# Expert layers of a transformer kernel: gate and up as three fp32r products instead of one fp32 product

## The reference

```
x = x + 0.5 * expert_ffn(layernorm(x))
x = x + attention(layernorm(x))
x = x + 0.5 * expert_ffn(layernorm(x))
x = x + 0.5 * sparse_ffn(layernorm(x))
x = x + mamba(layernorm(x))
x = x + 0.5 * sparse_ffn(layernorm(x))
```

```
logits = 30 * tanh(x @ w_gate / 30);  probs = softmax(logits)
weights = probs where the expert is among the token's top 2, else 0
for e in range(8):
    h = silu(x @ w1[e]) * (x @ w3[e])        # w1, w3: 256 x 512 ("gate" and "up")
    out = out + h @ w2[e] * weights[:, e]    # w2: 512 x 256 ("down")
```

## Time and profile before

| what | value |
|---|---|
| median of 3 runs | 1663.79 us (1658.72 to 1665.37) |
| the profiled execution | 1661.38 us, its span 1659.6 us |
| PE busy | 1454.4 us, 88% |
| DVE busy | 1085.8 us, 65% |
| ACT busy | 847.5 us, 51% |
| POOL busy | 487.5 us, 29% |
| mean granted TensorE clock | 0.938 of 2.4 GHz |
| the two expert layers, from first gate to last down | 137.7 and 137.8 us |

### The profile page before, as it was taken

One profiled execution on the slowest core, in us unless ns is written; L12 is line 12 of the kernel. 1 busy time (PEld: TensorE's weight loads), 2 busy tenths in 40 slices (PEclk: granted clock), 3 DMA queues, 4 the chain that ended last, 5 costly groups with the idle time before them and its releaser, 6 DMA issues. The chain is left out here.

```text
span 1659.6 us, 24358 instructions
## 1 busy us (share of the span) xinstructions
PE 1454.4 (88%) x7712; PEld 1014.0 (61%) x7712; DVE 1085.8 (65%) x1948; ACT 847.5 (51%) x1206; POOL 487.5 (29%) x407
## 2 busy tenths in 40 slices
PE   3999589999999976997697887899999999998697
PEld 2566443333333344664486776788887887887586
DVE  4122499999999843121676766787877778877475
ACT  1222227777777731221433767576666675765332
POOL 1344220000000112443100104756655656565100
PEclk7999769999999976999799989999999999999799
DMA  8522211111111028222201012222222222221200
GB/s 296 145 45 45 56 27 20 26 27 27 27 27 27 5 75 299 47 47 44 92 1 39 20 38 87 90 83 89 96 77 96 76 91 93 82 91 39 76 1 26
DMA packets 83007, 111.79 MB, mean 67 GB/s; under 512 B 11904, under 2 KB 60800, under 8 KB 82912
## 3 DMA queue, kind: packets, MB, share of 16 engines
q1 hardware_dynamic: 73152, 96.05, 19.3%
q0 software_dynamic: 9376, 14.16, 4.8%
q10 hardware_dynamic: 384, 0.39, 0.1%
HBM read 89.99 MB, written 11.93 MB: 61 GB/s over the span
## 5 line engine op out<-in xcount | busy, mean ns | idle before, releaser
L923 DVE TENSOR_REDUCE attn_max_chunks<-attn_scores 128x1 f32<-128x512 f32 x488 | 305.4, 684 | 22.9 <-PE attn_scores L1174 22.8
L1085 ACT ACTIVATE attn_probs<-attn_scoresT 128x1024 f32<-128x1024 f32 x256 | 248.0, 1022 | 111.9 <-PE attn_scoresT L1190 111.6
L1174 PE MATMUL attn_scores<-attn_k_picks,attn_q_group 64*128 64x512 f32 x488 | 185.8, 461 | 11.1 <-DVE attn_max_chunks L923 2.3
L1174 PEld LDWEIGHTS attn_scores<-attn_k_picks,attn_q_group 64*128 64x128 f32 x488 | 84.7, 189 | 172.6 <-DVE attn_max_chunks L923 163.9
L1605 DVE SCALAR_TENSOR_TENSOR ssm_scan_x<-ssm_scan_proj,ssm_w_conv,ssm_scan_x 128x1023 f32<-128x1023 f32 (+2 forms) x96 | 123.0, 1282 | 81.8 <-ACT ssm_scan_x L1600 75.4
L401 DVE TENSOR_TENSOR moe_h<-moe_silu,moe_up 128x512 f32<-128x512 f32 x46 | 31.6, 688 | 189.9 <-PE moe_up L516 189.9
L1190 PE MATMUL attn_scoresT<-attn_q_group,attn_k_picks 64*128 64x512 f32 x512 | 152.2, 435 | 3.2 <-ACT attn_probs L1085 3.2
L1202 PE MATMUL attn_o<-attn_probs,attn_v_group 128*32 128x512 f32 x1024 | 137.3, 608 | 0.4 <-ACT attn_probs L1085 0.3
L62 PE MATMUL ssm_scan_proj<-ssm_xnT_hi,ssm_w_in_hi 128*128 128x512 f32 x256 | 109.4, 427 | 23.7 <-DVE ssm_scan_x L1605 21.7
L448 ACT ACTIVATE moe_silu<-moe_gate 128x512 f32<-128x512 f32 x46 | 27.5, 598 | 200.9 <-PE moe_gate L516 200.9
L286 POOL DMA_INDIRECT moe_sums<-moe_y,moe_token x46 | 72.7, 1580 | 165.7 <-DVE moe_y L410 160.0
(11 more groups left out here) (339 smaller groups left out, 3092.4 us busy)
## 6 DMA issues: line engine op xcount, KB each, us to landing
ssm_cum_all<-ssm_cums SPq DMA_DIRECT2D x32, 512.0 KB, 3.8
ssm_scan_exp_cum<-ssm_cums SPq DMA_DIRECT2D x32, 512.0 KB, 3.7
moe_w_gate_up<-in_moe_w SPq DMA_DIRECT2D x16, 512.0 KB, 11.1
moe_w_up<-in_moe_w SPq DMA_DIRECT2D x16, 512.0 KB, 11.1
moe_w_down<-in_moe_w SPq DMA_DIRECT2D x16, 512.0 KB, 11.5
ssm_w_in<-in_in_w SPq DMA_DIRECT2D x64, 128.0 KB, 2.6
ssm_scan_w_out<-in_out_w SPq DMA_DIRECT2D x8, 512.0 KB, 3.8
moe_sums<-main_residual SPq DMA_DIRECT2D x2, 1024.0 KB, 5.6
```

Source lines behind the costliest of these rows:

```text
L923: return nc.vector.tensor_reduce(rmaxc[:, half, place:place + 1], chunk_bank(g, n), AX_X, ALU.max).then_inc(reduced, 1)
L1085: nc.scalar.activation(probs[s % 2][:, 2 * pair:2 * pair + 2, :], st_ps[pair][:], ACT.Exp, scale=SCALE).then_inc(exp_done, 1)
L1174: nc.tensor.matmul(chunk_bank(g, n), qs[b][head_rows(j), t * P:(t + 1) * P], kz[b][head_rows(j), j % 2, c * BANK:(c + 1) * BANK], start=Tr ...
```

## The change

The weights of gate and up are kept twice, as high and low parts in fp32r (`w_hi`, `w_lo`). SP's DMAs now write the raw weights into `w_lo`; ACT rounds them into `w_hi` (`high_weights`, two instructions of 128x1024 per expert), and DVE replaces the raw values by the difference, in place (`split_weights`, two of 128x1024 per expert). Experts 0 to 2 (`SPLIT_AHEAD`) are split before the first item, expert e from 3 to 7 at the end of ACT's and DVE's work of item e - 3. x is split for each item: ACT's copy out of PSUM now writes the high part, and DVE subtracts it from PSUM (`low_x`, 128x256), which PE waits for in place of ACT's copy. Gate and up become `matmul3`. To make room in SBUF, silu, h, hT, y, two of the four gathered row buffers and the parts of x lie in tiles of the router that are no longer used by then (xnT, xn, in_row), so in the order below moe_xnT, moe_xn and moe_in_row stand for them. The down product is unchanged.

```diff
+SPLIT_AHEAD = 3
...
-        w_in = {n: sp.sb(f"w_{n}", [P, EXPERTS * KD, INNER]) for n in ("gate_up", "up")}
+        w_hi = {n: sp.sb(f"w_{n}_hi", [P, EXPERTS * KD, INNER], F32R) for n in ("gate", "up")}
+        w_lo = {n: sp.sb(f"w_{n}_lo", [P, EXPERTS * KD, INNER], F32R) for n in ("gate", "up")}
...
-                for name, src in (("gate_up", w1), ("up", w3)):
-                    sync.dma_start(w_in[name][:, e * KD:(e + 1) * KD, :], src[e].rearrange("(k p) n -> p k n", p=P)
+                for name, src in (("gate", w1), ("up", w3)):
+                    sync.dma_start(f32(w_lo[name][:, e * KD:(e + 1) * KD, :]), src[e].rearrange("(k p) n -> p k n", p=P)
...
+            def split_weights(e):
+
+                for n, name in enumerate(("gate", "up")):
+                    own = slice(e * KD, (e + 1) * KD)
+                    dve.wait_ge(q["w_hi_done"], 2 * e + n + 1)
+                    nc.vector.tensor_tensor(w_lo[name][:, own, :], f32(w_lo[name][:, own, :]), f32(w_hi[name][:, own, :]),
+                                            ALU.subtract).then_inc(q["w_lo_done"], 1)
+
+            def low_x(i):
+                dve.wait_ge(q["xT_done"], i + 1)
+                nc.vector.tensor_tensor(xT_lo[i % 2][:], xT_ps[:, 0:D].rearrange("p (k n) -> p k n", k=KD), f32(xT_hi[i % 2][:]),
+                                        ALU.subtract).then_inc(q["xT_lo_done"], 1)
...
+            for e in range(SPLIT_AHEAD):
+                split_weights(e)
+            low_x(0)
             for i in range(ITEMS):
+                if i + 1 < ITEMS:
+                    low_x(i + 1)
                 product(i)
                 if i:
                     weigh(i - 1)
+                if i + SPLIT_AHEAD < EXPERTS:
+                    split_weights(i + SPLIT_AHEAD)
...
+            def high_weights(e):
+                act.wait_ge(expert_loaded[e], 48)
+                for name in ("gate", "up"):
+                    own = slice(e * KD, (e + 1) * KD)
+                    nc.scalar.copy(w_hi[name][:, own, :], f32(w_lo[name][:, own, :])).then_inc(q["w_hi_done"], 1)
...
+            for e in range(SPLIT_AHEAD):
+                high_weights(e)
             copy_x(0)
...
                 if i + 1 < ITEMS:
                     copy_x(i + 1)
+                if i + SPLIT_AHEAD < EXPERTS:
+                    high_weights(i + SPLIT_AHEAD)
...
             def project(i, e, name, bank, done):
                 for k in range(KD):
-                    last = nc.tensor.matmul(bank[:].unsqueeze(1), xT[i % 2][:, k, :], w_in[name][:, bass.ds(e * KD + k, 1), :],
-                                            start=(k == 0), stop=(k == KD - 1))
+                    own = bass.ds(e * KD + k, 1)
+                    last = matmul3(nc, bank[:].unsqueeze(1), (xT_hi[i % 2][:, k, :], xT_lo[i % 2][:, k, :]),
+                                   (w_hi[name][:, own, :], w_lo[name][:, own, :]), start=(k == 0), stop=(k == KD - 1))
                 last.then_inc(q[done], 1)
 
             def gate(i, e):
-                pe.wait_ge(q["xT_done"], i + 1)
+                pe.wait_ge(q["xT_lo_done"], i + 1)
...
                 if i < EXPERTS:
                     pe.wait_ge(expert_loaded[i], 48)
+                    pe.wait_ge(q["w_lo_done"], 2 * (i + 1))
```

More of the change, by code:

```diff
@@ L222, in moe_layer @@
         slot_w = sp.sb("slot_w", [P, COLS])
[L224 to L229, removed]
+        later = xnT[:].rearrange("p k n -> p (k n)")
+        g = [later[:, b * INNER:(b + 1) * INNER] for b in range(2)]
+        h = [later[:, (2 + b) * INNER:(3 + b) * INNER] for b in range(2)]
+        later = xn[:].rearrange("p t d -> p (t d)")
+        hT = [later[:, b * KI * P:(b + 1) * KI * P].rearrange("p (k n) -> p k n", k=KI) for b in range(2)]
+        y = [later[:, 2 * KI * P + b * D:2 * KI * P + (b + 1) * D] for b in range(2)]
+        xg = [sp.sb(f"x_rows{b}", [P, D])[:] for b in range(2)]
+        xg += [later[:, 2 * KI * P + b * D:2 * KI * P + (b + 1) * D] for b in range(2, 4)]
+        later = in_row[:].rearrange("p a n -> p (a n)")
+        xT_hi = [later[:, b * D:(b + 1) * D].rearrange("p (k n) -> p k n", k=KD) for b in range(2)]
+        xT_lo = [later[:, (2 + b) * D:(3 + b) * D].rearrange("p (k n) -> p k n", k=KD) for b in range(2)]
         gate_ps = [sp.ps(f"gate{b}", [P, BANK]) for b in range(2)]
@@ L242, in moe_layer @@
                  "row_done", "send_done", "slots_done", "expert_done", "token_done", "slot_w_done",
-                 "x_turned", "xT_done", "gate_done", "up_done", "silu_done", "h_done", "h_turned",
+                 "x_turned", "xT_done", "xT_lo_done", "w_hi_done", "w_lo_done", "gate_done", "up_done", "silu_done", "h_done", "h_turned",
                  "hT_done", "out_done", "y_done")
@@ L441, in copy_x @@
                     act.wait_ge(q["up_done"], i - 1)
-                nc.scalar.copy(xT[i % 2][:], xT_ps[:, 0:D].rearrange("p (k n) -> p k n", k=KD)).then_inc(q["xT_done"], 1)
+                nc.scalar.copy(xT_hi[i % 2][:], xT_ps[:, 0:D].rearrange("p (k n) -> p k n", k=KD)).then_inc(q["xT_done"], 1)
             def silu(i):
@@ L508, in turn_x @@
                 if i:
-                    pe.wait_ge(q["xT_done"], i)
+                    pe.wait_ge(q["xT_lo_done"], i)
                 for k in range(KD):
@@ L515, in project @@
                 for k in range(KD):
-                    last = nc.tensor.matmul(bank[:].unsqueeze(1), xT[i % 2][:, k, :], w_in[name][:, bass.ds(e * KD + k, 1), :],
-                                            start=(k == 0), stop=(k == KD - 1))
+                    own = bass.ds(e * KD + k, 1)
+                    last = matmul3(nc, bank[:].unsqueeze(1), (xT_hi[i % 2][:, k, :], xT_lo[i % 2][:, k, :]),
+                                   (w_hi[name][:, own, :], w_lo[name][:, own, :]), start=(k == 0), stop=(k == KD - 1))
                 last.then_inc(q[done], 1)
             def gate(i, e):
-                pe.wait_ge(q["xT_done"], i + 1)
+                pe.wait_ge(q["xT_lo_done"], i + 1)
                 if i >= 2:
                     pe.wait_ge(q["silu_done"], i - 1)
-                project(i, e, "gate_up", gate_ps[i % 2], "gate_done")
+                project(i, e, "gate", gate_ps[i % 2], "gate_done")
             def up(i, e):
```

## The result

| | before | changed |
|---|---|---|
| median of 20 runs | 1665.36 us | 1657.24 us (1644.03 to 1664.57) |
| ratio, 95% interval | | 0.9947, 0.9934 to 0.996 |
| profiled execution, span | 1661.4, 1659.6 us | 1655.5, 1653.7 us |

I had forecast 1632 us, with a range from 1625 to 1647. The median is 8 us faster than before, not 31, and lies above the range.

The account below looks back on a forecast made before the run. TensorE alone was taken to set the expert layers' pace. Saving 31.7 us in the items and adding 1.0 at the starts took 1661.4 us to 1630.7 (1633.1 from the median); forecast 1632 us, range 1625 to 1647.

Parts of the forecast that it names:

- The step that failed: Stages after the expert layers: nothing in the change touches them; the sum gave them no term.
- the sum: Whole kernel: -31.7 us in the items plus 1.0 at the starts, -30.7 us, 1661.4 to 1630.7 for the profiled execution.
- the sign: Expert layers: period 5.12 us while the time hardly moves would mean the time went to a stage after the layers.
- Saving in the loop: Gate and up per item: twelve fp32r products, 2.74 us, replace four fp32, 3.43 us; 0.69 us times 46, 31.7 us.
- Start: Before each expert layer's first gate: `low_x(0)` now stands between ACT's copy and gate, 0.5 us a layer, +1.0 in all.
- Rival 1: Layer start and loop: DVE's subtractions and POOL hold each other up, 4 to 8 us a layer, 1640 to 1647; chance 0.22.
- Rival 2: Gate and up: PE's sequencer can't feed 0.229 us products with register addresses; 1704 us (chance 0.04) or partly, 1642 (0.07).
- Rival 3: Expert items: POOL's chain of additions grows from 4.40 to over 5.12 us and becomes the bound, about 1645; chance 0.03.

Follow-up runs that it names:

- test 2: Kernel before, with 39 one-column memsets on DVE and 16 one-column copies on ACT behind each expert layer's last item: 1673.14 us, ratio 1.0034.
- test 4: Changed kernel with 89 memsets on DVE, 112 copies on ACT and 115 matmuls on PE added per expert layer, one column each: 1639.07 us, ratio 0.9833.
- test 5: Changed kernel with 89 one-column memsets on DVE per expert layer, nothing added on ACT and PE: 1643.63 us, ratio 0.9879.
- test 8: Changed kernel with 25 one-column memsets on DVE per expert layer: 1646.15 us, ratio 0.9895.
- test 9: Changed kernel with 57 one-column memsets on DVE per expert layer: 1649.19 us, ratio 0.9889.
- test 7: The kernel of test 4 with 39 more one-column memsets on DVE per expert layer: 1645.05 us, ratio 0.9887.
- test 3: Kernel before, with 141 one-column matmuls (282 instructions) on PE behind each expert layer's last down product: 1672.77 us, ratio 1.0034.
- test 6: Changed kernel with 115 one-column matmuls on PE per expert layer, nothing added on DVE and ACT: 1646.84 us, ratio 0.9889.
- test 1: Changed kernel once more, unchanged, for a second profile: 1654.47 us, ratio 0.9921.
- test 10: The kernel of test 8 again, unchanged, profiled once more: 1641.94 us, ratio 0.9862.
- test 12: Test 4 with only gate as three products, up one fp32 product without x's low part, pads to the same places: 1653.1 us, ratio 0.9922.
- test 11: Test 4 with weights split two experts ahead (SPLIT_AHEAD 2 in place of 3): 1639.14 us, ratio 0.9839.

## Why the prediction was wrong

**The step that failed** is the last one of the text, that a stage after the layers is one "which nothing here touches", and with it the silent assumption under the sum that a microsecond saved per item arrives at the end. The sum has no term for these stages, so they stood at nothing without a reason; they took 18.2 us, 6.6 in attention and 11.6 in mamba. The prediction had named the sign, a period near 5.12 us and a time that hardly moves. The sum counted added instructions only by the time that they run. They also move all code behind them. For DVE and attention this is shown: pads alone make the stall (test 2) and take it away (tests 4, 5, 8, 9), and it is back when the shift is a whole block more than the changed kernel's (test 7). It costs 182 - 175 = 7 us in two passes; the stage grew by 6.6.

For mamba, pads on PE alone bring a loss of the same size (test 3) and PE's pads take it away (test 6), but the place of PE's code does not decide it by itself: with the same PE code, test 8 has 662.8 us and test 9 has 675.7. Two things add up. The first is the loop, 2.5 us. Call an engine's code off a whole block where the shift ahead of the mamba loop (twice that of a layer) is no multiple of 128 on DVE or of 256 on PE. Over all fourteen profiles its nine packets and PE's stall are there in just the three in which both DVE's and PE's code are off a whole block at that place (the changed kernel, tests 1 and 9); with PE's alone off (tests 3, 5, 8, 10) there is neither. Why it takes both is not shown.

The second is the clock. About 8 us of the 11.6 had already come about in the first 150 us of the stage, before this loop. The first 62 us of the stage, changed, then before:

```profile
876.32:938.32 62.00, 52.65 (x260) 44.46 (x260) 39.51 (x55) 39.91 (x57) 6.91 (x7) 0.81 0.15 39
```

```profile
893.50:955.50 62.00, 51.36 (x287) 43.47 (x288) 43.27 (x58) 43.49 (x62) 8.19 (x8) 0.92 0.17 42
```

Neither DVE nor PE has an idle time of kind "issue" over 1.5 us there. The same products stand 0.43 us apart, as at 1.2 GHz, where they stood 0.23 apart before (changed, then before):

```profile
888.13 0.63 PE L62 MATMUL ssm_prep_proj<-ssm_xnT_hi,ssm_prep_w_bc_hi 128*128 128x512 f32 x1
888.56 0.63 PE L63 MATMUL ssm_prep_proj<-ssm_xnT_lo,ssm_prep_w_bc_hi 128*128 128x512 f32 x1
```

```profile
903.94 0.39 PE L62 MATMUL ssm_prep_proj<-ssm_xnT_hi,ssm_prep_w_bc_hi 128*128 128x512 f32 x1
904.17 0.40 PE L63 MATMUL ssm_prep_proj<-ssm_xnT_lo,ssm_prep_w_bc_hi 128*128 128x512 f32 x1
```

The delay against the kernel before, both counted from the start of the stage, grows by 0.4 us in the changed kernel with every two such products, to 5.2 us at the stage's 140th matmul and, after a second such stretch some 120 us into the stage (clock 0.91 from 994.70 to 1035.20, 1.00 at the same place before), to 8.0. In the fourteen profiles the delay at the 140th matmul goes with the granted clock of these 62 us: 0.92 in the kernel before, 0.89 with 0.5 to 0.8 us (tests 10 and 12), 0.86 with 2.7 to 2.8 (tests 4, 5, 8, 11), 0.81 with 4.9 to 5.5 (the changed kernel, tests 1, 2, 3, 6, 7, 9). All with 0.81 but test 3 have DVE's code off a whole block there, and no other profile has.

So the 8 us are time at the lower level of the clock. What makes the clock fall at another moment in these kernels stays open. In four of the seven profiles with PE's code off by the change's 282 instructions a layer they are there (the changed kernel, tests 1, 3 and 9), in the other three (tests 5, 8, 10) the same stretch grew by 1 to 3 us, and in the five with PE's code at a whole number of 256 (tests 4, 6, 7, 11, 12) by 1.5 to 4.4; in test 2, where PE has no added code, by 4.9.

The Trainium skill has the rule that I did not look for ("Runtime: NRT & Kernel Launch", section "Instruction fetch mechanics"): instructions stream through a small buffer in blocks, and a taken branch whose target is not in it stops the engine until the block is fetched. The trace agrees, with idle times of 2.65 to 2.8 us on DVE in the attention loop and 3.4 to 3.8 on PE in the mamba loop. The same section of the Trainium skill gives blocks of 16 KiB, 256 instructions, for every engine; here q8's packets have this size, but q14's have 8 KB, and DVE's stalls came back after 128 instructions, so the measurement decides. The Trainium skill gives a buffer of 512 instructions for most engines. By that, an estimate, a loop of 278 that touches three blocks of 128 fits with one block fetched ahead, and one that touches four does not; no run here shows the buffer's size. By the Trainium skill PE's buffer holds 2048, and the mamba loop has some 1640 records of PE per pass, so by that, an estimate, it too would be near the edge.

**The other terms**, in the profiled execution:
- *Saving in the loop*, forecast -31.7, measured -29.6. The distance between products is 0.235 us (56.10 to 57.28 is five of them), not the 0.229 of the FFN: twelve take 2.82 and the item saves 0.61. (The step behind gate's first product is 0.42 us, 55.68 to 56.10, but down, ahead of the next gate, takes 1.54 in place of 1.72, so the switch costs nothing over an item.) 46 x 0.61 = 28; the rest comes from the first items, where products stand 0.43 us apart (46.49 to 46.92 in the first gate).
- *Start*, forecast +0.5 a layer. From the last step of the router's list to the first gate it took 8.41 and 8.19 us before, 9.20 and 9.30 now: +0.8 and +1.1.

```profile
37.10 1.22 DVE L407 TENSOR_TENSOR moe_w_gate_lo<-moe_w_gate_lo,moe_w_gate_hi 128x1024 fp32r<-128x1024 f32 x1
37.77 1.47 POOL L283 DMA_INDIRECT moe_x_rows<-moe_rows,moe_token  x1 [20.61 <-DVE moe_token L398]
...
44.81 0.37 ACT L475 CAST moe_in_row<-moe_xT 128x256 fp32r<-128x256 f32 x1 [9.94 <-PE moe_xT L548]
45.22 0.42 DVE L412 TENSOR_TENSOR moe_in_row<-moe_xT,moe_in_row 128x256 fp32r<-128x256 f32 x1 [1.22 <-ACT moe_in_row L475]
45.90 0.79 PE L62 MATMUL moe_gate<-moe_w_gate_hi,moe_in_row 128*128 x1 [1.13 <-DVE moe_in_row L412]
```

  From copy to gate it is 1.09 us, 0.46 more than in the earlier trace rows, close to the forecast. The rest is the first gather, 1.47 us in place of 1.04, in the second layer 1.53 in place of 1.05.
- *Rival 1*: half right. The gathers beside subtractions take 1.47, 1.88 and 1.96 us, the subtractions 1.22 as I had taken. It costs 0.3 us in the first layer and 0.65 in the second, not 4 to 8. The rule of the Trainium skill on the shared port pair ("SBUF — State Buffer", section "SBUF: two separate sides") would have one wait out the other; here six subtractions ran back to back at unchanged length, so none waited for a gather, and the gathers beside them took 0.4 to 1.0 us longer, less than one subtraction. Whether a gather stood still for that time, as by the rule, or ran slower, the trace does not show. Of the additions in the loop, the first four took 2.2 to 2.3 us in place of 1.6, inside the period.
- *Rival 2* fell: apart from the step named above, the distances are 0.23 to 0.24 us. *Rival 3* fell: POOL's last two additions are still 4.4 us apart, within 5.20.
- The sum now: -29.6 + 1.9 + 6.6 + 11.6 + 3.1 (router) + 0.5 (all other stretches) = -5.9 us, from 1661.4 to 1655.5. With the code moved back to its places, the profiled execution of test 4 took 1639.8, 9.1 us above the sum's 1630.7: 1.8 are saving that the items lack, 3.0 start and router, 2.8 mamba, the rest is spread over the other stretches.

## What to carry to other kernels

Count an edit's instructions on each engine, and look for loops in the code behind it. Here the place of a loop's code alone decided whether 3.5 us were lost at each jump back on the engine that sets the pace; that a loop touching one block more is fetched again is the reading that fits, by four places tried. Look for it in the instruction queues' packets (more than the code's size) and in "issue" idle times just behind a branch. Then compare the granted clock of the stages behind: in mamba more of the loss came from there than from the stall. Before calling a change small, time it with a few dozen idle instructions in front of the next loop; comparing two kernels in one placement each can mistake the placement for the change.

## What was unexpected of the hardware

- Thirty-nine one-column instructions on DVE and 16 on ACT per layer make a kernel of 1666 us 7 us slower, and a further 89, 112 and 115 on DVE, ACT and PE make the changed one 15 us faster.
- DVE's instructions come in packets of 8 KB (q14), PE's in packets of 16 KB (q8). The two passes of the attention loop on DVE (278 records each) bring in one such packet at shifts 0, 64, 96 and 128, and eleven at 39 and 167.
- DVE standing for 3 us in the mamba loop need cost nothing: test 7 has such a stall at 1264.09 (3.29 us), and the pass is 133.7 us, shorter than the 135.5 of the kernel before, which had none; the clock of the two passes was 1.00 and 0.99.
